# Output projection of the layer stage: from an FP32 product to three fp32r products of split rows and split weights

## The chip, the cores and the metric

The kernel runs on one core of one Trainium2 chip. The metric is the time of one execution on the device in microseconds; the figures are the median, the lowest and the highest of several executions. A profile is one more execution, recorded instruction by instruction; its times are those of that one execution. TensorE, the matrix engine, is called PE, its weight loads PEld; VectorE is DVE, ScalarE is ACT, GpSimd is POOL, SyncE is SP.

## The reference

The input is x, 16 sequences of 512 rows of 256 values. Four blocks follow one another, each with `x = layernorm(x + block(x))`:

```python
x = layernorm(x + L0_attn(x))   # windowed softmax attention, 16 heads of 64
x = layernorm(x + L0_ffn(x))    # int8 product, scales, bias
x = layernorm(x + L1_attn(x))   # linear attention, then gelu
x = layernorm(x + L1_ffn(x))    # ternary weights + low rank; relu squared

# L1_attn, the block that the change is in; per sequence, 1024 features = 8 chunks of 128
q, k, v = x @ wq + bq, x @ wk + bk, x @ wv + bv
Q, K = elu(q) + 1, elu(k) + 1
KV, Ksum = sum_s(K * v), sum_s(K)
attn = Q * KV / (Q * Ksum + 1e-6)
out = gelu(attn @ wo + bo)      # [512, 1024] @ [1024, 256]
```

All of it is float32, and the output is compared as such.

## The kernel before

The program has two stages. The first does the attention of block 0 for all sequences and takes the first 2000 us; the change doesn't touch it. The second, `run_layers`, does everything else, and begins at about 2004 us. SBUF is laid out anew for each stage.

**Tiles.** A sequence is 512 rows. Features lie on the 128 partitions, rows on the free side, so that k, v, q and up products have the form "128 features x 512 rows" in one PSUM bank each. The 1024 features of block 1's attention are `HC` = 8 chunks, the 1024 hidden features of its FFN `FC` = 8 chunks.

**Split products.** Most products are float32 products in three passes of the one-pass type fp32r: an operand a is split as `hi = round(a)` (written to an fp32r tile) and `lo = a - hi`, and hi*hi + lo*hi + hi*lo is summed in PSUM. Weights are split once, rows each time: ACT writes hi, DVE or POOL subtracts lo. Two products differ. The down product's weights are exact in fp32r, so it takes two parts (`rhi`, `rlo` with `proj_t`). The output projection, `pe_out` (L1138 through `pe_rows_product`), multiplies plain float32 tiles `at` and `wo`; the profile records two weight loads and two matmuls for each of its instructions, 8 for one chunk.

**Order.** `all_steps` runs b from -3 to 18 and c from 0 to 7; each engine walks through these steps in program order and meets the others at semaphores only. In step (b, c) of the steady state PE does, in this order: the k and the v product of sequence b+1, chunk c-1; at c = 0 a transposition of the next rows (`pe_y2`); the q product of (b, c); the out product of (b, c-2); at c = 0 the second `pe_y2`; the up product of sequence b-2, chunk c; at c = 7 `pe_y3`; the down product; the int8 work of a later sequence at c = 1 to 3; at c = 7 the second `pe_y3`. So four sequences are under way at once. K_BANK, V_BANK (used by v and by up in turn) and Q_BANK are single banks: the next product waits until DVE has read the last.

DVE does per step: `dve_k` (L1330), `dve_v` (L1337), `dve_at` (L1359, one tensor_scalar from `z`), at c = 0 the small sums (L1343 to L1350) and the low part of y2 (L1326), `dve_q` (L1365, then L1369), at c = 3 the inner part of the gelu (L1390, L1392) and at c = 4, 5 its last product (L1396), then the square (L1377, from the ReLU), at c = 7 the low part of y3 (L1326). Sums, statistics and copies for other sequences stand at the head of the step: L1403 at c = 1, L1384 at c = 2, L1321 at c = 3, 4, statistics (L66 to L78) at c = 4 to 6, L1311 and L1313 at c = 7.

ACT does: the square's high part (L1254); at c = 1, 7 L1207 or a normalisation (L93); ReLU and exponential of k (L1217, L1219); `act_q_inverse` of (b, c-1) (L1237, L1240), which writes `z` as the logarithm's exponential; the same pair for q; at c = 3, 4 three gelu gate passes (L1263 to L1267); at c = 5, 6 a normalisation; the ReLU of the up product (L1247).

POOL does: the square's low part (L1492), which the down product waits for; a bias sum at c = 0 (L1461), two down sums at c = 1 (L1485), two gelu passes at c = 2 (L1472), int8 sums at c = 3, 4 (L1468), two gelu sums at c = 5 (L1479), and 128x4 powers for the normalisations (L85, L87) at c = 4 to 6.

**Memory.** `ring` has 16 slots of 512 columns: two each for `at`, `z`, `r`, `sq`, `uq`, `uk`, one each for `ek`, `eq`, two for `gx` (the out product with bias). A buffer pair lets a step's producer run while the step before is still read.

**Prologue.** Steps b = -3 to -1 load and prepare weights beside the first rows: the ternary FFN weights on DVE (`dve_weights`: L830 to L861), wq's split (ACT L1019, POOL L1039), the rank product (`dve_rank`, L868). DMA loads are issued by SP, and by ACT before its first step; `wo` is the last of ACT's, and the first out product waits for it.

## Time and profile before

| | us |
|---|---|
| median of 3 runs | 3261.58 |
| lowest, highest | 3256.11, 3261.69 |
| the profiled execution | 3256.74 |
| its span, first to last instruction | 3254.9 |
| PE busy | 3055.7 (94%) |
| PE weight loads busy | 2500.4 (77%) |
| DVE busy | 2319.4 (71%) |
| ACT busy | 2161.6 (66%) |
| POOL busy | 1480.8 (45%) |
| out product, L1138, 1024 records | 242.4 busy, 379 ns each |
| down product, L1138, 512 + 512 records | 131.0 and 128.4 busy, 288 and 283 ns each |
| L1359 (`at`), 128 times | 78.1 busy, 610 ns each |
| L1492 (square's low part), 128 times | 170.9 busy, 1335 ns each |

How to read it: busy time is the union of an engine's instructions. Matmuls are pipelined: the record of one lasts longer than the time after which the next one starts, so the cost of a product is read from start to start. DVE and ACT instructions overlap by some 0.08 us when they follow each other without a wait. "[x <-ACT ...]" behind a row is idle time of the engine before the instruction, and what ended it.

### The profile page before, as it was taken

How to read it: one execution, taken by the hardware profiler on the slowest of the kernel's cores; microseconds unless marked ns; L12 is line 12 of the kernel's file. 1: busy time of each engine (PE TensorE's matmuls, PEld its weight loads, DVE VectorE, ACT ScalarE, POOL GpSimd, SP SyncE). 2: the span in 40 equal slices, each digit the busy share in tenths (PEclk: the TensorE clock that was granted, in tenths of full speed). 3: DMA queues.
4: the chain of work that ended last, by engine and by line, in shares of the span. 5: the costliest groups of instructions: out<-in, count | busy, mean ns of one | idle time of the engine just before them, and what ended most of it. 6: DMA issues, size and time to landing. Idle time of an engine off the chain costs nothing. (4 is left out here: it accounts for less than half of the span.)

```text
span 3254.9 us, 68762 instructions
## 1 busy us (share of the span) xinstructions
PE 3055.7 (94%) x20655; PEld 2500.4 (77%) x20655; DVE 2319.4 (71%) x6737; ACT 2161.6 (66%) x5660; POOL 1480.8 (45%) x2090
## 2 busy tenths in 40 slices
...
GB/s 80 8 14 21 9 14 21 9 14 21 10 14 21 9 14 21 10 14 21 9 14 21 2 27 79 27 7 7 14 17 16 20 14 14 14 14 14 7 14 20
DMA packets 50143, 58.60 MB, mean 18 GB/s; under 512 B 2849, under 2 KB 47921, under 8 KB 49473
## 3 DMA queue, kind: packets, MB, share of 16 engines
...
## 5 line engine op out<-in xcount | busy, mean ns | idle before, releaser
L577 POOL TENSOR_SCALAR a_ex<-a_ex,a_rc 128x384 f32<-128x384 f32 (+1 forms) x1024 | 533.8, 535 | 749.7 <-DVE a_rc L489 749.5
L386 ACT ACTIVATE a_ex<-a_sm,a_nm 128x384 f32<-128x384 f32 (+1 forms) x1024 | 572.5, 560 | 100.3 <-DVE a_nm L482 97.4
L482 DVE CUSTOM_DVE_ANT_0 a_sm<-sc,a_mask,a_rn 128x384 f32<-128x384 f32 (+1 forms) x1024 | 532.0, 545 | 45.3 <-PE sc L267 43.1
L1492 POOL TENSOR_TENSOR b_rlo<-b_ring,b_rhi 128x512 fp32r<-128x512 f32 x128 | 170.9, 1335 | 586.3 <-ACT b_rhi L1254 586.1
L392 ACT ACTIVATE a_pt<-tp 128x256 f32<-128x256 f32 (+1 forms) x512 | 220.1, 430 | 304.6 <-PE tp L278 304.6
L236 PE MATMUL pj<-a_whi,a_xhi 128*128 128x384 f32 x1024 | 397.1, 388 | 2.5 <-DVE a_rb L460 2.5
L561 POOL TENSOR_TENSOR a_qr<-a_ra,a_rb 128x256 f32<-128x256 f32 x512 | 367.5, 733 | 35.8 <-DVE a_rb L460 35.7
L267 PE MATMUL sc<-a_kT,a_qT 64*128 64x384 f32 (+1 forms) x2048 | 345.3, 455 | 2.4 <-DVE a_nm L482 0.9
L236 PE MATMUL pj<-a_whi,a_xlo 128*128 128x384 f32 x1024 | 346.4, 338 | 0.0
L236 PE MATMUL pj<-a_wlo,a_xhi 128*128 128x384 f32 x1024 | 345.2, 337 | 0.0
L288 PE MATMUL qk<-a_pt,a_v 128*64 128x128 f32 x5120 | 314.6, 278 | 31.7 <-issue 21.4
L288 PEld LDWEIGHTS qk<-a_pt,a_v 128*64 128x64 f32 x5120 | 285.8, 139 | 68.8 <-issue 66.8
L494 DVE COPY a_pt<-sc 128x256 f32<-128x256 f32 (+1 forms) x512 | 250.9, 490 | 58.5 <-PE sc L278 51.6
L458 DVE TENSOR_TENSOR a_ra<-pj,a_cos 128x256 f32<-128x256 f32 x512 | 215.1, 420 | 57.9 <-ACT a_sq L371 51.7
L267 PEld LDWEIGHTS sc<-a_kT,a_qT 64*128 64x128 f32 x2048 | 176.3, 186 | 96.0 <-issue 53.5
L278 PE MATMUL sc<-s_ident,a_ex 128*128 128x128 f32 x1280 | 232.2, 279 | 11.5 <-DVE a_pt L494 6.2
L1138 PE MATMUL out<-b_wo,b_ring 128*128 128x256 f32 x1024 | 242.4, 379 | 0.2 <-DVE b_ring L1384 0.2
L278 PE MATMUL tp<-s_ident,a_ex 128*128 128x128 f32 x1280 | 228.9, 277 | 4.8 <-ACT a_pt L392 4.1
L297 PE MATMUL qk<-a_wo,a_ot 128*128 128x256 f32 x1024 | 228.0, 381 | 1.5 <-DVE a_res L502 0.8
L1330 DVE SCALAR_TENSOR_TENSOR b_ring<-k,b_one_bk,b_ring 128x512 f32<-128x512 f32 x128 | 95.8, 748 | 178.0 <-ACT b_ring L1219 178.0
L297 PEld LDWEIGHTS qk<-a_wo,a_ot 128*128 128x128 f32 x1024 | 192.0, 190 | 35.1 <-issue 8.2
L1138 PEld LDWEIGHTS out<-b_wo,b_ring 128*128 128x128 f32 x1024 | 194.4, 190 | 31.3 <-issue 0.6
...
## 6 DMA issues: line engine op xcount, KB each, us to landing
...
```

The source lines that it names most:

```text
L236: last = e.matmul(PJ[t % 2][:, 0:3 * PW], a[:, c, t * P:(t + 1) * P], w[:, c, p * 3 * PW:(p + 1) * 3 * PW], start=c == 0 and k == 0, stop= ...
L267: e.matmul(SC[j][h][:, 0:width], qT[par][rows(h), (w + j) * WS:(w + j + 1) * WS], kT[par][rows(h), lo * WS:(hi + 1) * WS], start=True, sto ...
L278: last = e.transpose(TPS[h][:, k * P:(k + 1) * P], ex[h][w][:, k * P:(k + 1) * P], ident[:, :])
L288: last = e.matmul(QK[rows(h), w * WS:(w + 1) * WS], v[p % 4][:, k, rows(h)], pt[h][w][:, (k - lo) * P:(k - lo + 1) * P], start=k == lo, st ...
L297: last = e.matmul(QK[:, t * DIM:(t + 1) * DIM], ot[:, c, (2 * k + t) * P:(2 * k + t + 1) * P], wo[:, c, :], start=c == 0, stop=c == HC - 1)
L386: e.activation(ex[h][w][:, 0:width], sm[h][w % 2][:, 0:width], ACT.Exp, bias=nm[:, w, h:h + 1], scale=-1.0, accum_out=rs[:, w, h:h + 1]).t ...
L392: e.activation(pt[0][w][:, 0:width], TP[:, 0:width], ACT.Copy).then_inc(g['pt_act'], 1)
L482: e.tensor_tensor_reduce(out=sm[h][w % 2][:, 0:width], in0=SC[w % 2][h][:, 0:width], in1=mem['mask'][:, off:off + width], scale=rn[:, par, ...
L494: e.tensor_copy(pt[1][w][:, 0:width], TPS[1][:, 0:width]).then_inc(g['pt_dve'], 1)
L561: e.tensor_tensor(qr[par][:, t, :], ra[:, t % 2, :], rb[:, t % 2, :], ALU.add).then_inc(g['rot_pool'], 1)
L577: e.tensor_scalar(row, row, 0.0, rc[:, w, h:h + 1], ALU.add, ALU.mult).then_inc(g['exn_pool'], 1)
L1138: last = e.matmul(bank[:, t % 2 * DIM:(t % 2 + 1) * DIM], xt[:, t * P:(t + 1) * P], weight[:, c, :], start=c == 0 and t % 2 == 0 and k == ...
```

## The change

The output projection is computed as the other split products are: `at` is split into `ahi` and `alo`, `wo` into `wo_hi` and `wo_lo`, and a chunk's product takes three parts, 12 fp32r matmuls in place of 4 float32 ones.

- DVE computes `at` twice from `z`: once into `ahi` (fp32r) and once into `at` (float32). POOL subtracts: `alo = at - ahi` (`pool_at_low`), in each step, behind most of the step's other POOL work. PE waits for POOL's event instead of DVE's.
- `wo` is loaded into four ring slots and split in the prologue, in four pieces: ACT writes `wo_hi`, POOL `wo_lo`.
- The two new weight tiles and four new row tiles take memory. To make room, `at`, `z`, `r`, `uq`, `uk` get one buffer instead of two, `gx` and `dn` share one place, and prologue buffers move. Each brings a wait.
- `dve_rank` moves from step (-1, 3) to (-1, 6). In POOL's step the rstd of ln3 comes ahead of `pool_at_low`, the gelu's inner part behind it.

```diff
     def dve_rank(e):
+        e.wait_ge(w['wq_pool'], 4)
...
         if (b, c) == (-1, 3):
             dve_fc_difference(e)
-            dve_rank(e)
...
+        if (b, c) == (-1, 6):
+            dve_rank(e)
...
     def act_weights(e, b, c):
+        if out_weights_piece(b, c) is not None:
+            act_out_weights(e, out_weights_piece(b, c))
...
+    def out_weights_piece(b, c):
+        steps = ((-2, 7), (-1, 0), (-1, 5), (-1, 6))
+        return steps.index((b, c)) if (b, c) in steps else None
...
+    def act_out_weights(e, n):
+        e.wait_ge(i['wo'], 16)
+        e.activation(out_columns('wo_hi', n), out_columns('wo_raw', n), ACT.Copy).then_inc(w['wo_act'], 1)
+
+    def pool_out_weights(e, n):
+        e.wait_ge(w['wo_act'], n + 1)
+        e.tensor_tensor(out_columns('wo_lo', n), out_columns('wo_raw', n), out_columns('wo_hi', n).bitcast(F32),
+            ALU.subtract).then_inc(w['wo_pool'], 1)
...
     def pe_out(e, s, c):
-        e.wait_ge(g['at_dve'], HC * s + c + 1)
+        e.wait_ge(g['al_pool'], HC * s + c + 1)
         if (s, c) == (0, 0):
-            e.wait_ge(i['wo'], 16)
+            e.wait_ge(w['wo_pool'], 4)
             e.wait_ge(w['bu_dve'], 2)
         if c == 0 and due(s):
             e.wait_ge(g['o_dve'], 2 * s)
-        pe_rows_product(e, O, [(mem['at'][c % 2], mem['wo'])], c).then_inc(g['o_pe'], 1)
+        hi, lo = (mem['ahi'][c % 2], mem['alo'][c % 2])
+        pe_rows_product(e, O, [(hi, mem['wo_hi']), (lo, mem['wo_hi']), (hi, mem['wo_lo'])], c).then_inc(g['o_pe'],
+            1)
...
     def act_q(e, s, c):
         e.wait_ge(g['q_pe'], HC * s + c + 1)
+        if (s, c) == (0, 0):
+            e.wait_ge(w['wo_pool'], 4)
...
     def act_q_inverse(e, s, c):
-        if due(n - 1):
-            e.wait_ge(g['at_dve'], n - 1)
+        if due(n):
+            e.wait_ge(g['at_dve'], n)
...
     def act_relu(e, s, c):
-        if due(n - 1):
-            e.wait_ge(g['sq_dve'], n - 1)
+        if due(n):
+            e.wait_ge(g['sq_dve'], n)
...
     def dve_k(e, s, c):
         e.wait_ge(g['ke_act'], HC * s + c + 1)
+        if due(HC * s + c):
+            e.wait_ge(g['v_dve'], HC * s + c)
...
     def dve_at(e, s, c):
         if due(n - 1):
             e.wait_ge(g['o_pe'], n - 1)
-        e.tensor_scalar(mem['at'][c % 2], mem['z'][c % 2], mem['nc'][:, c:c + 1], mem['cc'][:, c:c + 1], ALU.mult,
-            ALU.add).then_inc(g['at_dve'], 1)
+        factor, term = (mem['nc'][:, c:c + 1], mem['cc'][:, c:c + 1])
+        e.tensor_scalar(mem['ahi'][c % 2], mem['z'], factor, term, ALU.mult, ALU.add)
+        if due(n):
+            e.wait_ge(g['al_pool'], n)
+        e.tensor_scalar(mem['at'], mem['z'], factor, term, ALU.mult, ALU.add).then_inc(g['at_dve'], 1)
...
     def dve_q(e, s, c):
-        if due(n - 1):
-            e.wait_ge(g['ql_act'], n - 1)
+        if due(n):
+            e.wait_ge(g['ql_act'], n)
...
     def dve_out_bias(e, s, k):
+        if k == 0 and due(s - 1):
+            e.wait_ge(g['y4_pool'], 2 * (s - 1))
...
+    def pool_at_low(e, s, c):
+        n = HC * s + c
+        e.wait_ge(g['at_dve'], n + 1)
+        if due(n - 1):
+            e.wait_ge(g['o_pe'], n - 1)
+        e.tensor_tensor(mem['alo'][c % 2], mem['at'], mem['ahi'][c % 2].bitcast(F32),
+            ALU.subtract).then_inc(g['al_pool'], 1)
...
     def pool_step(e, b, c):
-        if c == 2 and inside(b - 1):
-            for k in range(2):
-                pool_gelu_inner(e, b - 1, k)
...
+        if c == 6 and inside(b - 1):
+            n3.rstd(e, b - 1)
+        if inside(at[0]):
+            pool_at_low(e, *at)
+        if c == 2 and inside(b - 1):
+            for k in range(2):
+                pool_gelu_inner(e, b - 1, k)
         if c == 5 and inside(b + 2):
             n2.rstd(e, b + 2)
-        if c == 6 and inside(b - 1):
-            n3.rstd(e, b - 1)
+        if out_weights_piece(b, c) is not None:
+            pool_out_weights(e, out_weights_piece(b, c))
...
-            e.dma_start(mem['wo'][:, :, :], io['wo1'].rearrange('(c p) n -> p c n', p=P)).then_inc(i['wo'], 16)
+            e.dma_start(mem['wo_raw'], io['wo1'].rearrange('(c p) n -> p c n', p=P)).then_inc(i['wo'], 16)
...
-    for i, k in enumerate(('at', 'z', 'r', 'sq', 'uq', 'uk')):
-        mem[k] = [ring[:, 2 * i + j, :] for j in range(2)]
-    mem['ek'], mem['eq'] = (ring[:, i, :] for i in (12, 13))
-    mem['gx'] = ring[:, 14:16, :]
+    for i, k in enumerate(('at', 'z', 'uq', 'eq', 'r')):
+        mem[k] = ring[:, i, :]
+    mem['sq'] = [ring[:, i, :] for i in (5, 6)]
+    mem['uk'], mem['ek'] = (ring[:, i, :] for i in (7, 8))
+    mem['gx'] = mem['dn'] = ring[:, 9:11, :]
```

## Rows read from the trace of the kernel before

**Rows 1.** Busy time by stretch: start:end, length, engines (instructions), PE clock, DMA, GB/s.
```profile
2397.42:2469.68 72.26, 70.35 (x355) 58.24 (x354) 48.59 (x117) 55.62 (x90) 25.58 (x24) 1.00 0.05 15
```

**Rows 2.** Waits of PE in that stretch: us in total, times, longest.
```profile
PE v_up L1058 <- DVE b_ring L1377: 1.1, 1, 1.1
PE t L1052 <- DVE b_y3lo L1326: 0.6, 1, 0.6
PE v_up L1058 <- DVE b_ring L1337: 0.2, 1, 0.2
```

**Rows 3.** Order in time on PE, step (5, 3): start, us, engine, line, operation.
```profile
2428.28 1.89 PE L1138 MATMUL out<-b_wo,b_ring 128*128 128x256 f32 x8
...
2430.24 0.40 PE L1058 MATMUL v_up<-b_y3lo,b_fhi 128*128 128x512 f32 x1
...
2431.50 0.28 PE L1138 MATMUL down<-b_proj_t,b_rlo 128*128 128x256 f32 x1
2431.62 0.28 PE L1138 MATMUL down<-b_proj_t,b_rhi 128*128 128x256 f32 x1
```

**Rows 4.** Order in time on DVE and POOL, three places where they meet.
```profile
3158.30 1.50 DVE L1365 TENSOR_SCALAR b_ring<-b_ring 128x512 f32<-128x512 f32 x1
3156.80 2.72 POOL L1479 TENSOR_TENSOR b_y<-b_g,b_y 128x512 f32<-128x512 f32 x2
...
2037.10 0.88 DVE L843 SCALAR_TENSOR_TENSOR b_dn<-b_y,b_wst,b_g 128x256 f32<-128x256 f32 x2
2037.50 1.95 DVE L843 SCALAR_TENSOR_TENSOR b_dn<-b_y,b_wst,b_g 128x256 f32<-128x256 f32 x2
2037.87 1.29 POOL L1039 TENSOR_TENSOR b_wq_lo<-b_y,b_wq_hi 128x512 fp32r<-128x512 f32 x1 [8.81 <-ACT b_wq_hi L1019]
...
2460.81 0.69 DVE L1313 TENSOR_SCALAR b_qf<-b_qf 128x1024 f32<-128x1024 f32 x1
2460.86 1.79 POOL L1492 TENSOR_TENSOR b_rlo<-b_ring,b_rhi 128x512 fp32r<-128x512 f32 x1 [5.03 <-ACT b_rhi L1254]
```

**Rows 5.** Order in time: L1365 in step (5, 3), and how soon POOL follows DVE.
```profile
2429.86 0.43 DVE L1365 TENSOR_SCALAR b_ring<-b_ring 128x512 f32<-128x512 f32 x1 [0.74 <-ACT b_ring L1219]
...
2451.57 0.17 DVE L78 TENSOR_SCALAR b_ln_ve<-b_ln_mv 128x4 f32<-128x4 f32 x1
2451.81 1.02 POOL L85 TENSOR_TENSOR b_ln_rs<-b_ln_ve,b_half 128x4 f32<-128x4 f32 x1 [4.09 <-DVE b_ln_ve L78]
```

**Rows 6.** Order in time on DVE and PE, step (5, 0).
```profile
2401.96 0.55 DVE L1359 TENSOR_SCALAR b_ring<-b_ring,b_nc,b_cc 128x512 f32<-128x512 f32 x1
2402.42 0.20 DVE L1343 RECIPROCAL b_ki<-b_su 128x8 f32<-128x8 f32 x1
...
2402.68 0.17 DVE L1346 TENSOR_TENSOR b_kb<-b_kb,b_kv 128x8 f32<-128x8 f32 x1
...
2403.16 0.68 DVE L1326 TENSOR_TENSOR b_y2lo<-t,b_y2hi 128x512 fp32r<-128x512 f32 x1
...
2403.90 0.66 PE L1052 MATMUL t<-s_ident,b_y 128*128 128x128 f32 x4
```

**Rows 7.** Order in time on DVE and PE, step (5, 7).
```profile
2466.73 0.43 DVE L1365 TENSOR_SCALAR b_ring<-b_ring 128x512 f32<-128x512 f32 x1 [0.69 <-ACT b_ring L1219]
...
2468.53 0.68 DVE L1326 TENSOR_TENSOR b_y3lo<-t,b_y3hi 128x512 fp32r<-128x512 f32 x1
...
2469.27 0.66 PE L1052 MATMUL t<-s_ident,b_y 128*128 128x128 f32 x4 [0.63 <-DVE b_y3lo L1326]
```

**Rows 8.** The square on DVE: all from 2200 to 3000 us, and in step (5, 4).
```profile
L1377 DVE SCALAR_TENSOR_TENSOR b_ring<-v_up,b_ring 128x512 f32<-128x512 f32 x88 | 60.8, 691 | 59.4 <-ACT b_ring L1247 59.4
...
2442.51 0.69 DVE L1377 SCALAR_TENSOR_TENSOR b_ring<-v_up,b_ring 128x512 f32<-128x512 f32 x1 [0.20 <-ACT b_ring L1247]
```

**Rows 9.** The load of wo: kind, count, KB and us to landing; and its issue.
```profile
b_wo<-wo ACTq DMA_DIRECT2D x1, 1024.0 KB, 12.4
...
2010.10 1.16 ACTq L1570 DMA_DIRECT2D b_wo<-wo  x1
```

More of the change, by code:

```diff
@@ L1040, in pool_query_weights, with out_columns @@
             ALU.subtract).then_inc(w['wq_pool'], 1)
+    def out_weights_piece(b, c):
+        steps = ((-2, 7), (-1, 0), (-1, 5), (-1, 6))
+        return steps.index((b, c)) if (b, c) in steps else None
+    def out_columns(name, n):
+        rows = mem[name] if name == 'wo_raw' else mem[name][:, :, :]
+        return rows.rearrange('p c n -> p (c n)')[:, n * 512:(n + 1) * 512]
+    def act_out_weights(e, n):
[5 more added lines that the diff above has]
+            ALU.subtract).then_inc(w['wo_pool'], 1)
     def pool_begin(e):
@@ L1233, in act_q_inverse @@
         e.wait_ge(g['qu_dve'], n + 1)
-        if due(n - 1):
-            e.wait_ge(g['at_dve'], n - 1)
-        z = mem['z'][c % 2]
-        e.activation(z, mem['uq'][c % 2], ACT.Ln, bias=mem['eps'][:, 0:1],
+        if due(n):
+            e.wait_ge(g['at_dve'], n)
+        z = mem['z']
+        e.activation(z, mem['uq'], ACT.Ln, bias=mem['eps'][:, 0:1],
             scale=mem['su'][:, s % 2, c:c + 1]).then_inc(g['ql_act'], 1)
@@ L1244, in act_relu @@
         e.wait_ge(g['h_pe'], n + 1)
-        if due(n - 1):
-            e.wait_ge(g['sq_dve'], n - 1)
-        e.activation(mem['r'][c % 2], V_BANK[:, :], ACT.Relu).then_inc(g['r_act'], 1)
+        if due(n):
+            e.wait_ge(g['sq_dve'], n)
+        e.activation(mem['r'], V_BANK[:, :], ACT.Relu).then_inc(g['r_act'], 1)
     def act_square_high(e, s, c):
@@ L1376, in dve_square @@
             e.wait_ge(g['rl_pool'], n - 1)
[L1377 removed]
+        e.scalar_tensor_tensor(mem['sq'][c % 2], V_BANK[:, :], 0.0, mem['r'], ALU.max,
             ALU.mult).then_inc(g['sq_dve'], 1)
@@ L1495, in pool_step @@
     def pool_step(e, b, c):
-        square = square_unit(b, c)
+        square, at = (square_unit(b, c), at_unit(b, c))
         if inside(square[0]):
@@ L1587, in sb @@
         return stack.enter_context(nc.sbuf_tensor('b_' + name, shape, dt))
-    mem = {k: sb(k, v) for k, v in dict(wo=[P, HC, DIM], ring=[P, 16, S], y1=[P, TT, DIM], qf=[P, TT, DIM], ws=[P,
-        DIM], bo=[P, DIM], bias=[P, DIM], psc=[P, DIM], g1=[P, 2, S], g2=[P, 2, S], dn=[P, 2, S], half=[P, TT],
+    mem = {k: sb(k, v) for k, v in dict(ring=[P, 11, S], y1=[P, TT, DIM], qf=[P, TT, DIM], ws=[P,
+        DIM], bo=[P, DIM], bias=[P, DIM], psc=[P, DIM], g1=[P, 2, S], g2=[P, 2, S], half=[P, TT],
         eps=[P, 1], ln_eps=[P, 1], unround=[P, 1], xs=[P, 2], top=[P, 2], gate=[P, 1], wst=[P, 4, FC], nbq=[P, HC],
@@ L1601, in layers_memory @@
     mem['y3hi'], mem['y3lo'] = (sb(k, [P, DC, S], F32R) for k in ('y3hi', 'y3lo'))
-    for k in ('rhi', 'rlo'):
+    for k in ('rhi', 'rlo', 'ahi', 'alo'):
         mem[k] = [sb(f'{k}{i}', [P, S], F32R)[:, :] for i in range(2)]
+    mem['wo_hi'], mem['wo_lo'] = (sb(k, [P, HC, DIM], F32R) for k in ('wo_hi', 'wo_lo'))
     mem['w8raw'] = sb('w8raw', [P, DC, DIM // 4], INT32)
```

35 lines of the change are left out of this document (17 added, 18 removed).

## The prediction

> **What bounds the kernel now.** I read the view by stretches first, for the layers, which are all that the change touches. One sequence, from one k product at step c = 0 to the next, takes 72.26 us; in it PE is busy 70.35, DVE 48.59, ACT 55.62, POOL 25.58, and the granted clock is 1.00, the 2.4 GHz level [rows 1]. The reader is to see a PE that hardly rests and a POOL with two thirds of its time free. Then the waits of PE in that sequence: 1.9 us in three places, always for DVE: a v product waits for the square, a transposition for the low part of y3, an up product for the v reduction [rows 2]. So PE is the bound, but at three points of each sequence a chain through ACT and DVE is just as long as PE's work. What is won or lost on those chains counts as much as what PE wins.
>
> **What PE gains.** The out product starts at 2428.28 and the second matmul behind it at 2430.24 [rows 3]. A matmul of 512 columns takes 0.23 (twice the 0.12 between two records of the down product, which have 256 columns [rows 3]), so one out product takes 2430.24 - 0.23 - 2428.28 = 1.73 us. The new one is 12 matmuls of the form of the down product: 12 x 0.12 = 1.43. Gain 0.30 us, 128 times: 38 us if nothing else moved.
> The Trainium skill (FP8 and Floating Point Precision, on FP32) says that true FP32 takes four passes through the array. By that the old product would be 16 x 0.12 = 1.92 us and the gain 0.49; the row says 1.73, and the row decides.
>
> **What DVE gets.** `dve_at` becomes two tensor_scalar passes instead of one. One more costs 0.47: L1359 starts at 2401.96 and its follower at 2402.42 [rows 6]. No row shows a tensor_scalar that writes fp32r. The nearest, a tensor_tensor that does, lasts 0.68, with the same overlap of 0.08 that is 0.60 [rows 6]; so the bounds are 0.47 and 0.60. I take 0.47, since operation and operands are L1359's. Behind the old pass DVE idles 0.74 us until ACT's exponential of q is there, and then runs L1365 [rows 5]. The second pass fits into that gap, and by itself costs little.
>
> **What POOL gets, and the lock.** One 128x512 subtraction per chunk, 1.29 us like L1039 [rows 4]. POOL has the time. But the trace shows that POOL and DVE shut each other out. L1365, else 0.43, took 1.50 while two L1479 ran on POOL until 3159.52; it ended 0.28 after them [rows 4]. L843, which has two SBUF inputs, takes 0.88 for two, and took 1.95 for two when L1039 held POOL until 2039.16; it ended 0.29 after it. The other way round, POOL's L1492 took 1.79 when it began 0.05 behind DVE's L1313 [rows 4]. Whoever starts first keeps the other out.
> The Trainium skill (SBUF — State Buffer, Who interferes with whom) calls it an exclusive lock on the second port pair, between GpSimd and a DVE instruction in a two-port mode or with two SBUF inputs. The trace agrees: 1.50 beside 0.43.
>
> Now the race in each step. POOL starts 0.07 to 0.08 us after the end of the DVE instruction that releases it (L78 ends at 2451.74, L85 starts at 2451.81) [rows 5]. L1365 starts when ACT is ready. Times from the end of the old pass:
> - Step 3. The second pass ends at +0.47, POOL starts at +0.55, L1365 would come at +0.74 [rows 5]: too late. POOL ends at +1.84, L1365 at +2.12 instead of +1.17: shift 0.95. Behind it lie q, the inner part of the gelu, ACT's three gate passes, the ReLU and the square, for which PE's v product of step 4 already waits 1.1 us [rows 2]. Cost +0.95, and the 0.30 of steps 3 and 4 turn into waiting.
> - Step 7. L1365's idle time is 0.69, so POOL wins again. From 2466.73 on DVE has 0.43, 0.75 and 0.69 us of work without a gap, then L1326 at 2468.53 (low part of y3), for which PE's transposition waits until 2469.27 [rows 7]. Cost +0.95.
> - Step 0. Behind the pass stand the small sums. L1346 (two SBUF inputs) started 0.17 after L1359's end [rows 6]; now POOL starts 0.08 after the second pass and holds it until 1.37 after it. Shift 0.47 + 1.37 - 0.17 - 0.15 of L1346's own length, 1.52. L1326 behind it (low part of y2) ended at 2403.84, PE's transposition started at 2403.90 [rows 6]. PE now waits: +1.52, and this product's 0.30 is gone.
> - Steps 1 and 2. L1365 is late by 1.0 too, but its square has idle time before it (0.67 on average over the steps [rows 8]) and PE comes to the v product only after down and k, over 2 us of work. No cost; the two gains stay: -0.60.
> - Step 4. DVE has no idle time there: L1365 follows at once and beats POOL. But POOL's subtraction then runs into L1396 (two SBUF inputs), and the square after it has 0.20 of idle time [rows 8]. 0.47 for the pass plus up to 0.5 for the lock, less 0.20, and step 5, where POOL's two L1479 come later for the same reason, hands it on to PE's v product of step 6. Bounds 0 and 1.0; I take +0.5.
> - Steps 5 and 6. Nothing new; their gains go into a chain of ACT (three normalisations) that ends in step 7's wait.
> Sum: 1.52 - 0.60 + 0.95 + 0.50 + 0.95 = +3.3 us, so 72.3 becomes 75.6.
>
> **The other edits.** Single buffers for z, uq, uk, r and at: each new wait is for something a whole step old (72.26 / 8 = 9 us) or already waited for on the same engine; that step hides it: 0. gx on dn's memory: DVE's L1384, and k and v behind it, wait for POOL's down sum of the step before, 2.6 us of its 9: 0; without that cover up to 1.3 once a sequence. POOL's order: the rstd of ln3 stays ahead of the subtraction, the gelu's part goes behind it and is needed a step later: 0. PE waits for POOL instead of DVE, but one step after the pass: 0.
> The split of wo adds 4 ACT and 4 POOL passes to the prologue. Its DMA lands 12.4 us after its issue at 2010.10 [rows 9], before ACT is through with the first rows. The last two POOL passes meet L861 and L1311, which are DVE work of the locking kind, at a time when DVE is the bound; `dve_rank` costs the same at its new place, and the q splits that it waits for are done by then. Bounds -1.3 (the rank copies leave a tight place) and +2.6 (two POOL passes in full, 2 x 1.29); I take +1.5.
>
> **Sum.** 13 full sequences (b = 2 to 14) x 3.3 = 43. The first two, without up and down: up to 14 gains of 0.30 against one step 0 and one step 7: +2 (-2 to +5). The last, with long waits for DVE: +3 (0 to +6). Prologue +1.5. Together +50 on the profiled execution's 3256.7: 3307. The median shown, 3261.6, lies 4.9 above that execution; I put half of it on top: **3309 us**.
> If a pass that writes fp32r takes 0.60, POOL starts at +0.68 and L1365 in step 7 (0.69) draws level: that term goes, 13 x 0.95 = 12 us: 3297. With all bounds at the upper end (13 x 0.5 + 7): 3322.
>
> **Rivals.**
> 1. *The lock costs nothing on the path* (POOL wakes later, or DVE is let in first): step 0 keeps +0.47 and the two gains -0.60: -0.13 per sequence, prologue and ends as above, 3257 to 3264: no change. Against it: L1365 at 1.50.
> 2. *The second pass hides in step 0 too*: 13 x 0.60 to 0.90 less the prologue: 3248 to 3254, faster.
> 3. *PE is the bound throughout*, its 1.9 us of waits only leftovers: 3261.6 - 38 = 3223. Against it: the three waits end chains in which no out product stands.
> By the four passes of the page named above this rival would give 128 x 0.49 less, 3199.
> 4. *The change doesn't do what it says*: the 12 matmuls go at the old product's 0.216, since weight loads show: 2.6 us, +0.86 in 2 to 4 steps, with the lock and without the gains 3337 to 3360. Against it: the down product has such loads at a pace of 0.12.
> The sign hangs on one point: whether POOL's subtraction starts within 0.27 us of the second pass's end in step 3.
>
> **Chances.** Forecast (3285 to 3326) 0.70; the lock in some steps only (3268 to 3285) 0.07; rival 1 0.09; rival 2 0.06; rival 3 0.04; rival 4 0.04. A measurement of this kernel tells about 0.2% (6.5 us) from no change. Faster 0.12, within 0.08, slower 0.80. The range leaves out rivals 2, 3 and 4 and half of rival 1: 3262 to 3326; the forecast's own is 3285 to 3326.
>
> **What would show it.** L1365's successor at about 1.4 us in steps 1, 2, 3, 6 and 7 and at 0.43 in steps 4 and 5; an out product of 1.43 us; a sequence of 75 to 76 us; waits of PE of about 1 us or more in steps 0 and 7 and 2 in step 4. I am wrong if L1365 keeps 0.43 in step 3, or a sequence takes under 73 us.

## The result

| | before | after |
|---|---|---|
| median | 3258.85 (3253.94 to 3261.69, 4 executions) | 3315.94 (3314.98 to 3316.87, 4 executions) |
| profiled execution, its span | 3256.74, 3254.9 | 3316.87, 3315.1 |

After to before: 1.0177, 95% interval 1.0159 to 1.0194. The change costs 57 us. The prediction was 3309, range 3262 to 3326, slower with 0.80.

**One sequence.** A sequence is read as the stretch from PE's k product at the head of one step (b, 0) to the next, as in [rows 1]. In the trace of after it is b = 4 and b = 5, and two microseconds within b = 5 (columns as in [rows 1]: length; busy time and count of PE, PEld, DVE, ACT, POOL; granted clock):

```profile
2343.26:2419.06 75.80, 68.12 (x387) 58.01 (x386) 57.80 (x125) 55.46 (x90) 36.44 (x32) 1.00 0.05 15
2419.06:2495.53 76.47, 69.44 (x387) 59.06 (x386) 59.06 (x125) 55.48 (x90) 36.05 (x32) 0.98 0.05 14
2461.00:2463.00 2.00, 2.00 (x6) 1.52 (x6) 1.93 (x9) 1.17 (x2) 1.82 (x2) 0.50 0.00 0
```

Against [rows 1] PE does 2.2 us less in b = 4 (70.35 to 68.12), DVE 9.2 more, POOL 10.9 more, and the sequence is 3.5 us longer. The second row has a part that no row of before had between b = 2 and 14: the granted clock falls to 0.50 for a few microseconds.

**Which step.** The steps of b = 4, one row each:

```profile
2343.26:2354.06 10.80, 9.14 (x55) 7.82 (x54) 7.30 (x17) 6.28 (x10) 4.60 (x3) 1.00 0.01 2
2354.06:2362.42 8.36, 8.36 (x54) 7.28 (x53) 6.27 (x11) 6.12 (x9) 5.10 (x4) 1.00 0.00 0
2362.42:2370.80 8.38, 8.38 (x52) 7.27 (x50) 6.84 (x13) 7.11 (x11) 3.89 (x4) 1.00 0.00 0
2370.80:2379.17 8.37, 8.37 (x52) 7.27 (x49) 5.91 (x11) 4.64 (x7) 3.84 (x3) 1.00 0.01 2
2379.17:2390.32 11.15, 8.54 (x48) 6.96 (x45) 9.37 (x25) 9.25 (x15) 5.18 (x5) 1.00 0.15 47
2390.32:2398.24 7.92, 7.92 (x46) 6.89 (x45) 6.51 (x13) 6.74 (x12) 5.20 (x4) 1.00 0.01 2
2398.24:2407.49 9.25, 8.19 (x46) 6.82 (x45) 7.76 (x28) 6.79 (x13) 5.23 (x6) 1.00 0.17 58
2407.49:2419.06 11.57, 9.22 (x54) 7.70 (x53) 7.84 (x13) 8.54 (x15) 3.41 (x3) 1.00 0.00 1
```

In steps 1, 2, 3 and 5 PE is busy all the time (8.38 of 8.38): there it is the bound, and there the cheaper product shows. In 0, 4, 6 and 7 its busy time is 1 to 2.6 us less than the step. Cut the same way, the kernel before (b = 5, the stretch of [rows 1]) has 9.32, 8.65, 8.66, 8.66, 9.92, 8.24, 8.42, 10.39; its steps 0, 3, 4, 6 and 7:

```profile
2397.42:2406.74 9.32, 9.32 (x51) 7.76 (x50) 5.81 (x16) 6.28 (x10) 3.33 (x2) 1.00 0.00 0
...
2424.05:2432.71 8.66, 8.66 (x48) 7.36 (x45) 5.71 (x12) 5.18 (x8) 2.56 (x2) 1.00 0.01 2
2432.71:2442.63 9.92, 8.85 (x44) 6.89 (x41) 7.98 (x23) 8.71 (x15) 3.78 (x4) 1.00 0.17 53
...
2450.87:2459.29 8.42, 8.42 (x43) 6.91 (x41) 6.21 (x25) 6.84 (x12) 3.68 (x5) 1.00 0.19 64
2459.29:2469.68 10.39, 9.55 (x50) 7.64 (x49) 6.47 (x12) 8.27 (x15) 2.12 (x2) 1.00 0.00 1
```

So steps 1, 2, 3 and 5 won 0.3 each, and 0, 4, 6 and 7 lost 1.5, 1.2, 0.8 and 1.2. Step 6 of b = 4 is longer than most: its median from b = 2 to 13 is 8.91, so that it usually loses 0.5.

**For whom PE waits.** Waits of PE in b = 4 (total, times, longest), to be held against [rows 2]:

```profile
PE v_up L1079 <- DVE b_ring L1407: 3.3, 2, 2.3
PE t L1073 <- DVE b_y2lo L1351: 1.7, 1, 1.7
PE t L1073 <- DVE b_y3lo L1351: 1.6, 1, 1.6
PE v_up L1079 <- DVE b_ring L1364: 1.1, 2, 0.8
```

L1407 is the square (L1377 before), L1351 the low parts (L1326), L1364 `dve_v`. 1.9 us of waiting have become 7.7, all of it for DVE, as before. The wait for y2's low part, in step 0, and a second one for the square, in step 6 (1.1 us here), are new; none is for POOL.

**The lock.** Step 3 of b = 4: the two passes, POOL's subtraction (L1524), and the first operation on q (L1395, L1365 before) with its successor:

```profile
2375.33 0.55 DVE L1387 TENSOR_SCALAR b_ahi<-b_ring,b_nc,b_cc 128x512 fp32r<-128x512 f32 x1
2375.79 0.54 DVE L1390 TENSOR_SCALAR b_ring<-b_ring,b_nc,b_cc 128x512 f32<-128x512 f32 x1
2376.61 1.37 DVE L1395 TENSOR_SCALAR b_ring<-b_ring 128x512 f32<-128x512 f32 x1 [0.28 <-ACT b_ring L1242]
2378.02 0.75 DVE L1399 SCALAR_TENSOR_TENSOR b_ring<-q,b_one_bq,b_ring 128x512 f32<-128x512 f32 x1
...
2376.41 1.29 POOL L1524 TENSOR_TENSOR b_alo<-b_ring,b_ahi 128x512 fp32r<-128x512 f32 x1 [2.10 <-DVE b_ring L1390]
```

L1390 ends at 2376.33, POOL starts 0.08 later, L1395 comes 0.20 behind POOL and lasts 1.37 instead of 0.43, until 0.28 after POOL's end. In step 5 DVE is first and POOL is the one that is drawn out:

```profile
2396.11 0.53 DVE L1390 TENSOR_SCALAR b_ring<-b_ring,b_nc,b_cc 128x512 f32<-128x512 f32 x1
2396.57 0.41 DVE L1395 TENSOR_SCALAR b_ring<-b_ring 128x512 f32<-128x512 f32 x1
...
2396.72 1.41 POOL L1524 TENSOR_TENSOR b_alo<-b_ring,b_ahi 128x512 fp32r<-128x512 f32 x1 [0.81 <-DVE b_ring L1390]
```

In step 0 it is one of the small sums that is held (L1373, `kb + kv`, 8 columns: 1.20 us), and behind it the low part of y2 for which PE waits 1.7 us. The first sum with two SBUF inputs, L1371, still slipped in 0.05 ahead of POOL:

```profile
2348.26 0.54 DVE L1390 TENSOR_SCALAR b_ring<-b_ring,b_nc,b_cc 128x512 f32<-128x512 f32 x1
2348.72 0.20 DVE L1370 RECIPROCAL b_ki<-b_su 128x8 f32<-128x8 f32 x1
2348.83 0.12 DVE L1371 TENSOR_TENSOR b_kb<-b_su,b_bv 128x8 f32<-128x8 f32 x1
2348.98 1.20 DVE L1373 TENSOR_TENSOR b_kb<-b_kb,b_kv 128x8 f32<-128x8 f32 x1
...
2348.88 1.27 POOL L1524 TENSOR_TENSOR b_alo<-b_ring,b_ahi 128x512 fp32r<-128x512 f32 x1 [2.29 <-DVE b_ring L1390]
```

Over the program L1395 has 411/1368/1462 ns (lowest, median, highest); L1365 had a median of 427. The out product is 12 matmuls 0.12 apart:

```profile
2394.82 0.28 PE L1159 MATMUL out<-b_wo_hi,b_ahi 128*128 128x256 f32 x1
...
2395.78 0.28 PE L1159 MATMUL out<-b_wo_lo,b_ahi 128*128 128x256 f32 x1
```

(The second row is its ninth.) The Trainium skill (SBUF — State Buffer, Who interferes with whom) lets whoever issues first keep the shared port pair for its whole instruction; these three places agree, in both directions.

**The clock.** The v product of step 4, now in b = 5 (PE's rows; the bracket is the wait before the instruction and its releaser):

```profile
2458.90 0.50 PE L1079 MATMUL v_up<-b_y2hi,s_w_hi 128*128 128x512 f32 x1 [2.28 <-DVE b_ring L1407]
2459.24 0.39 PE L1079 MATMUL v_up<-b_y2lo,s_w_hi 128*128 128x512 f32 x1
...
2460.79 0.63 PE L1079 MATMUL q<-b_y2hi,b_wq_hi 128*128 128x512 f32 x1
2461.22 0.63 PE L1079 MATMUL q<-b_y2lo,b_wq_hi 128*128 128x512 f32 x1
```

About a microsecond after a wait of 2.28 us the matmuls start 0.43 apart instead of 0.23: the granted clock is 0.50 (1.2 GHz) for some 3.4 us. In b = 4 the same wait of 2.28 stands there and no fall follows. Between b = 2 and 14 eight sequences have such a stretch, and each begins between 0.3 us before and 1.5 us after the end of that wait (2.69 us in b = 14). Step 4 then lasts 12.0 to 12.1 instead of 11.15. q is late by it; in five of the eight, b = 5 among them, L1395 then comes so late (0.42 after the second pass) that POOL wins in step 4 too. That adds little: in b = 11 POOL doesn't win, and step 4 lasts 12.1 all the same.

**Where the 60 us of the two profiles lie** (the layers' start is SP's first load there, the other borders are the k products at (0, 0), (2, 0) and (15, 0)): the attention stage, whose code is the same, ends 5.1 later; the layers' start to (0, 0) 63.0 to 65.5, +2.5; the first two sequences 113.8 to 116.6, +2.7; the 13 full ones 936.5 to 985.8, +49.3; the end 136.7 to 137.2, +0.6.

### The profile page after: what moved, and what is told of

It reads as the page before. It is cut to its first block and busy times, and to the rows that moved or that the text cites. A ratio compares the mean times of both kernels' runs of the same rounds, so it can differ in the third digit from the quotient of the medians.

```text
span 3315.1 us, 70305 instructions
## 1 busy us (share of the span) xinstructions
PE 3037.6 (92%) x21167; PEld 2509.0 (76%) x21167; DVE 2469.6 (74%) x6865; ACT 2161.4 (65%) x5664; POOL 1651.5 (50%) x2222
## 5 line engine op out<-in xcount | busy, mean ns | idle before, releaser
L1524 POOL TENSOR_TENSOR b_alo<-b_ring,b_ahi 128x512 fp32r<-128x512 f32 x128 | 169.5, 1325 | 276.1 <-DVE b_ring L1390 276.1
L460 DVE TENSOR_TENSOR a_rb<-pj,a_sin 128x256 f32<-128x256 f32 x512 | 211.9, 414 | 0.0
```

## The experiments

Columns: the median of one sequence (b = 2 to 13), and the steps in that order, all by PE's k products. "Total" is one execution where no ratio stands beside it, and else a median and its ratio to the kernel before, run beside it.

| | 0 | 1 | 2 | 3 | 4 | 5 | 6 | 7 | sequence | total |
|---|---|---|---|---|---|---|---|---|---|---|
| before | 9.3 | 8.7 | 8.7 | 8.7 | 9.9 | 8.2 | 8.4 | 10.4 | 72.2 | 3259 |
| e4: old product, new buffers | 9.3 | 8.7 | 8.7 | 8.7 | 9.9 | 8.2 | 8.4 | 10.4 | 72.2 | 3259.8 |
| e3: new product alone | 9.3 | 8.4 | 8.4 | 8.4 | 10.2 | 7.9 | 8.4 | 10.6 | 71.7 | 3255.7 |
| e1: and the second pass | 9.8 | 8.4 | 8.4 | 8.4 | 10.2 | 7.9 | 8.6 | 10.6 | 72.3 | 3261.9 |
| e2: and POOL's subtraction | 10.1 | 8.4 | 8.4 | 8.4 | 10.4 | 7.9 | 9.1 | 10.9 | 73.5 | 3275.5 |
| after: both | 10.8 | 8.4 | 8.4 | 8.4 | 11.2/12.1 | 7.9 | 8.9 | 11.6 | 75.5/76.5 | 3316 |
| e7: PE's wait filled | 10.8 | 8.4 | 8.4 | 8.4 | 11.2 | 7.9 | 8.9 | 11.6 | 75.5 | 3308.3 |
| e8: after, old product | 10.8 | 8.6 | 8.7 | 8.7 | 10.9/12.1 | 8.3 | 8.9 | 11.3 | 76.0/77.0 | 3324.5 |
| e5: POOL behind q | 9.8 | 8.4 | 8.4 | 8.4 | 11.2/12.1 | 7.9 | 8.7 | 10.6 | 73.4/74.2 | 3290.0, 1.0081 |
| e9: and behind the gelu's inner part | 9.8 | 8.4 | 8.4 | 8.4 | 10.2 | 7.9 | 8.9 | 10.6 | 72.5 | 3266.9, 1.0014 |

(With a slash: without and with a fall of the clock in the sequence.)

### Which part costs what: e1 to e4

Without POOL's subtraction (e1):

```diff
-        if inside(at[0]):
-            pool_at_low(e, *at)
...
-        e.wait_ge(g['al_pool'], HC * s + c + 1)
+        e.wait_ge(g['at_dve'], HC * s + c + 1)
...
-        hi, lo = (mem['ahi'][c % 2], mem['alo'][c % 2])
+        hi = lo = mem['ahi'][c % 2]
```

> The changed kernel without POOL's subtraction of the row remainder; DVE keeps both passes, and the product takes the high part twice, so it has the same twelve matmuls. What is left out: the low part of the rows. Read from the full sequences b = 2 to 14 (before 72.3 us, after 75.8 with an undisturbed clock). Theory (the lock between POOL and DVE is the larger part of the loss): nothing holds L1395 (0.43 everywhere) nor the small sums of step 0. What is left is the second pass alone: step 0 +0.47, steps 1 and 2 -0.58, steps 3 and 4 about +0.47 and +0.2, step 7 +0.47, together about +1.0: 73.3 us a sequence, and some 3280 us in all. Rival A (the second pass is the loss, or the rate of DVE's work as a whole): stays at 75 to 76. Rival B (the second pass hides everywhere once the lock is gone): 71.7 us.

72.29 us, 3261.9 in all: less than expected. The 0.47 of the pass shows in step 0 (9.31 to 9.77, against e3) and 0.18 in step 6, but not in 3 and 7. That expectation had an error of its own: L1395 comes 0.7 us after the old pass, and the second pass fits into that gap. The lock is needed for the pass to cost anything there. L1395 (L1393 in e1) stays at 409 to 430 ns throughout. Rival A falls, and so does rival B, since step 0 does pay for the pass.

Without the second pass (e2), POOL subtracting `ahi` from itself:

```diff
-        e.tensor_scalar(mem['ahi'][c % 2], mem['z'], factor, term, ALU.mult, ALU.add)
-        if due(n):
-            e.wait_ge(g['al_pool'], n)
-        e.tensor_scalar(mem['at'], mem['z'], factor, term, ALU.mult, ALU.add).then_inc(g['at_dve'], 1)
+        e.tensor_scalar(mem['ahi'][c % 2], mem['z'], factor, term, ALU.mult, ALU.add).then_inc(g['at_dve'], 1)
```

> The changed kernel without DVE's second pass: POOL subtracts the high part from itself, as long a pass as before, 0.08 us after the first pass of DVE. What is left out: the low part of the rows is zero. Theory (lock): POOL still gets in ahead of L1395 in steps 3 and 7, where it comes 0.7 us after the pass, and ahead of the small sums in step 0; each loss is smaller by the 0.47 of the pass: step 0 +1.05, steps 1 and 2 -0.58, step 3 +0.48, step 4 about +0.2, step 7 +0.48 (to +0.7), together +1.6 to +1.9: 74.0 us a sequence, L1395's successor at 1.3 to 1.5 in steps 1, 2, 3, 6 and 7. Rival A (the second pass is the loss): 72 us or less.

73.54 us. Steps 0, 4, 6 and 7 are longer than in e3, as expected, but less so, and rival A (72 us or less) falls. Step 3 of b = 5:

```profile
2440.06 0.66 DVE L1392 TENSOR_SCALAR b_ring<-b_ring 128x512 f32<-128x512 f32 x1 [0.74 <-ACT b_ring L1242]
...
2439.40 1.04 POOL L1521 TENSOR_TENSOR b_alo<-b_ahi 128x512 fp32r<-128x512 f32 x1 [1.64 <-DVE b_ahi L1387]
```

With the same tile on both sides POOL took 1.04, not 1.29, so this run understates the lock by 0.25 in each held step. L1392 (L1395 of after) lasted 0.66: held 0.23, and again until 0.28 after POOL's end. With 1.29 the delay would have been 0.48, as expected; that is an estimate, not a run. The other sign that was named was missed: L1392 was put at 1.3 to 1.5 us in steps 1, 2, 3, 6 and 7, and has medians of 0.65 to 0.75 there. Without the second pass POOL starts 0.66 ahead of it in step 3, not 0.20, and most of POOL's operation is over when it comes.

Neither (e3: both edits together, the first pass and the three-part product left), and the old product on top (e4):

```diff
-        pe_rows_product(e, O, [(hi, mem['wo_hi']), (lo, mem['wo_hi']), (hi, mem['wo_lo'])], c).then_inc(g['o_pe'],
+        pe_rows_product(e, O, [(hi.bitcast(F32), mem['wo_hi'][:, :, :].bitcast(F32))], c).then_inc(g['o_pe'],
```

> The changed kernel with neither the second pass nor POOL's subtraction: the cheaper product (high part of the rows in both places), the single buffers, the new order of POOL and the split of the weights in the prologue stay. What is left out: the low part of the rows. Theory: only steps in which PE is the bound give their 0.3 us back, two to three of eight: 71.5 us a sequence (71.2 to 71.7), in all 3250 us with the prologue's loss. Rival C (PE is the bound throughout and its waits are leftovers): 72.3 - 2.4 = 69.9 us a sequence. Together with the two kernels before, the pass and the lock add up or don't: if their costs are a plain sum, after = this + (e1 - this) + (e2 - this).

> As the kernel before in its work per step (one FP32 product, one pass of DVE, no subtraction of POOL), but with the single buffers, the shared memory of gx and dn, POOL's new order and the split of the weights: the edits that the prediction costed at nothing in the sequences, and the prologue. What is left out: the low parts of rows and weights. Theory: 72.3 us a sequence as before (72.2 to 72.5), the prologue +1.5 to +2.5: about 3260 us in all. Rival D (one of the new waits of the single buffers or of gx counts): 73 to 74 us a sequence, and a new releaser in the waits of PE or ACT.

One sequence of e4, e3, e1 and e2, in this order, each from its own trace:

```profile
2403.29:2475.50 72.21, 70.32 (x355) 58.23 (x354) 48.52 (x117) 55.60 (x90) 25.57 (x24) 1.00 0.05 15
```

```profile
2403.19:2474.86 71.67, 68.15 (x388) 57.97 (x386) 48.56 (x117) 55.62 (x90) 25.59 (x24) 1.00 0.05 15
```

```profile
2406.71:2479.00 72.29, 68.10 (x387) 58.00 (x386) 52.20 (x125) 55.61 (x90) 25.61 (x24) 1.00 0.05 15
```

```profile
2407.39:2480.93 73.54, 68.11 (x387) 57.97 (x386) 51.36 (x117) 55.62 (x90) 34.06 (x32) 1.00 0.05 15
```

e4 repeats [rows 1] within 0.1 in every column: the single buffers, the shared place of gx and dn and POOL's order cost nothing, and rival D falls. From e4 to e3 PE's work drops by 2.2 us and the sequence by 0.54: the rest turned into waits of steps 4 (9.9 to 10.2) and 7 (10.4 to 10.6). Rival C, PE as the bound throughout, falls. From e3, the pass adds 0.6, POOL's subtraction 1.9, and both together 3.8 (75.5 - 71.7). They are no plain sum. 0.25 in each held step is POOL's shorter operation in e2. The rest follows from the starts, though no run shows it by itself: the pass alone is hidden in front of L1395, but it puts off POOL's start by 0.47, and with it the end of the lock.

The same question with one part instead of three (e11, `[(hi, mem['wo_hi'])]` in e3's kernel):

> The kernel with the product alone, its product cut from three parts to one (4 matmuls, 0.48 us, instead of 12, 1.43). What is left out: the low parts of rows and weights. Theory (PE is the bound only in steps 1, 2, 3 and 5): the gain of 0.95 stays in steps 1 and 2 as far as ACT allows (some 6.9 us of ACT a step), those of steps 3 and 5 turn into waits of steps 4 and 7 for the square: 71.65 - 1.9 = 69.7 to 70.5 us a sequence. Rival C (PE is the bound throughout): 71.65 - 7.6 = 64.0.

Two sequences have 70.4 us, as expected; the other ten have 71.0 to 73.0, mean 71.8, 3248.9 in all. Rival C (64.0) falls once more. 0.95 us less per product is worth nothing in the mean (71.8 beside e3's 71.7): PE waits 2.28 us for the square in step 4 and 1.90 for `dve_v` in step 7, and in b = 5, with 72.6 us, the clock fell behind both:

```profile
2437.83 0.50 PE L1079 MATMUL v_up<-b_y2hi,s_w_hi 128*128 128x512 f32 x1 [2.28 <-DVE b_ring L1404]
...
2468.81 0.72 PE L1079 MATMUL v_up<-b_y3hi,b_fhi 128*128 128x512 f32 x1 [1.90 <-DVE b_ring L1364]
```

The changed kernel with the old product (e8, the diff of e4 alone):

> The changed kernel with all work of DVE and POOL, but PE makes one FP32 product of the high parts, 1.73 us instead of 1.43. What is left out: the low parts of rows and weights. Theory: the 0.3 us count only in steps 1, 2, 3 and 5 and are taken off the waits of steps 4 and 7, as between the kernels with and without the new product (72.23 to 71.65): +0.6 us a sequence beside the changed kernel, 76.4 with an undisturbed clock, and shorter waits of PE (2.28 falls to about 2.0), with which the clock may fall less often. Rival C (PE is the bound): +2.4 us a sequence, 78.2 or more.

76.0 us without a fall, 77.0 with one: +0.5, as from e3 to e4. Steps 1, 2, 3, 5 are longer by 0.3, 4 and 7 shorter by 0.3. The product's gain is real and has the same size with the lock as without it.

### The clock: e7

```diff
     def pe_v(e, s, c):
+        if inside(s - 3) and c == 3:
+            e.wait_ge(g['qu_dve'], HC * (s - 1) + 4)
+            for k in range(8):
+                e.matmul(Q_BANK[:, :], mem['wq_hi'][:, 0, 0:P], mem['y2hi'][s % 2][:, 0, :], start=True, stop=True)
         if inside(s - 3):
```

> The changed kernel, with 8 matmuls (128x128 by 128x512, 0.23 apart, 1.85 us) of no use into q's bank, ahead of the v product of step 4, where PE otherwise waits 2.28 us for the square; q's own product overwrites them. Theory F (the granted clock falls to 0.50 in half of the sequences because of this wait, and that is what lengthens step 4 from 11.15 to 12.1): no stretch at 0.50 between b = 2 and 14, step 4 at 11.15 in all, the period 75.5 to 75.8 in all, some 6 us less in all, although PE has more to do. Rival G (the fall comes from elsewhere, and the waits only go beside it): stretches at 0.50 stay, median of step 4 near 12.

Step 4 of b = 5, PE:

```profile
2451.98 2.01 PE L1145 MATMUL q<-b_y2hi,b_wq_hi 128*128 128x512 f32 x8
2454.42 0.50 PE L1079 MATMUL v_up<-b_y2hi,s_w_hi 128*128 128x512 f32 x1 [0.43 <-DVE b_ring L1411]
```

But for one at the very start of b = 2 (at 2188.5, in the step's first microsecond) there is no stretch at 0.50 between b = 2 and 14. Nearly every sequence takes 75.5 us (75.47 to 75.52 in ten of twelve), step 4 is 11.16 throughout, and the program took 3308.3: eight useless matmuls a sequence made it faster, by 6.8 us in the 13 full sequences (985.8 to 979.1). Theory F holds: the wait is what brought the clock down, and rival G falls. Why only about every second wait does so is left open. It also gives the clean price of the change: 979.1 - 936.5 = 42.6 for 13 sequences.

### Where POOL may stand: e5, e6, e9, e10, e12

```diff
     def pool_at_low(e, s, c):
         n = HC * s + c
         e.wait_ge(g['at_dve'], n + 1)
+        if inside((n + 1) // HC):
+            e.wait_ge(g['qu_dve'], n + 2)
```

> The whole change, with one more wait: POOL's subtraction starts only when DVE's second operation on q (L1399) of the same step is done. Nothing is left out. Theory (what costs is that POOL gets in ahead of L1395 and of the small sums of step 0): L1395 takes 0.43 everywhere, step 0 is 9.77, steps 1 to 3 8.38, step 4 10.2, step 7 10.6 as in the kernel with the pass alone, 72.3 to 72.8 us a sequence (POOL may still get between the passes of the inner part of the gelu in step 3, where the square has 1.45 us of idle time), 3262 to 3268 in all, about the time of the kernel before. Rival E (any subtraction of POOL costs, wherever it stands, since 1.3 us of the ports are taken from DVE eight times a sequence): 74 us or more, 3285 and above.

L1395 takes 410 to 430 ns in all 128 cases, steps 0 and 7 are those of e1 (9.8, 10.6), and the kernel costs 28 us more than the kernel before run beside it (3262.2), where after cost 57. But step 4 is 11.2, and 12.1 with a fall of the clock, not 10.2. Step 3 of b = 5 in e5:

```profile
2448.53 0.68 DVE L1422 TENSOR_TENSOR b_g<-b_g,b_ring 128x512 f32<-128x512 f32 x1
2449.24 1.39 DVE L1424 TENSOR_SCALAR b_g<-b_g 128x512 f32<-128x512 f32 x1
...
2448.74 1.61 POOL L1526 TENSOR_TENSOR b_alo<-b_ring,b_ahi 128x512 fp32r<-128x512 f32 x1 [3.04 <-issue]
```

POOL, first held by L1422, gets in between it and L1424, which is held to 1.39. ACT's gate, the ReLU and the square come 0.96 later, PE's v product waits 2.30, and in eight of the twelve sequences the clock falls. By its numbers (74 us or more, 3285 and above) rival E fits this run better than the theory. Otherwise the theory was wrong by one place where the same lock bites again. One more wait tells these apart (e9):

```diff
+        if c == 2 and inside(s - 1):
+            e.wait_ge(g['gc_dve'], 4 * s)
```

> The run with POOL's subtraction behind q, and in step 3 alone it also waits for the last L1424 (the inner part of the gelu). Nothing is left out. Theory (in the run before, step 4 was 12.1 instead of 10.2 because the subtraction of step 3 started between L1422 and L1424, held L1424 to 1.39 instead of 0.43, and ACT's gate, the ReLU and the square behind it came 0.96 later; PE's 2.30 us of waiting then brought the clock down): L1424 back at 0.43, the v product of step 4 waits about 1.35, no stretch at 0.50 between b = 2 and 14, step 4 at 10.2 to 10.5, 72.3 to 72.6 us a sequence, 3262 to 3268 in all, within 0.3% of the kernel before. Rival E (any subtraction costs): step 4 stays at 11 or more, 73.4 us a sequence or more.

Its step 3:

```profile
2444.89 0.68 DVE L1422 TENSOR_TENSOR b_g<-b_g,b_ring 128x512 f32<-128x512 f32 x1
2445.61 0.43 DVE L1424 TENSOR_SCALAR b_g<-b_g 128x512 f32<-128x512 f32 x1
...
2447.32 1.27 POOL L1528 TENSOR_TENSOR b_alo<-b_ring,b_ahi 128x512 fp32r<-128x512 f32 x1 [5.24 <-DVE b_g L1424]
```

72.5 us a sequence, step 4 at 10.2, 3266.9 in all, ratio 1.0014 (1.0003 to 1.0024). The clock falls at the very start of b = 2 and once in b = 14 and nowhere between. POOL does the same 36.5 us of work a sequence as in after. All work of the change is there, and two waits of POOL have brought its cost from 57 to 6 us, each against the kernel before run beside it (the ratio from 1.0177 to 1.0014): it is where POOL's subtraction stands that costs. Rival E falls.

e9 lies 0.85 us a sequence above e3, all in steps 0 and 6; 0.46 and 0.18 of it are the second pass, as in e1. In e6 POOL makes the unrounded rows as well (0.77 to 1.0 us, in front of its subtraction), and `nc` and `cc` have two buffers:

```diff
     def pool_at_low(e, s, c):
...
+        e.tensor_scalar(mem['at'], mem['z'], mem['nc'][:, s % 2, c:c + 1], mem['cc'][:, s % 2, c:c + 1], ALU.mult,
+            ALU.add).then_inc(g['ap_pool'], 1)
+        e.wait_ge(g['ap_pool'], n + 1)
         e.tensor_tensor(mem['alo'][c % 2], mem['at'], mem['ahi'][c % 2].bitcast(F32),
```

> The whole change, with the subtraction behind q as in the run beside it, and the pass that makes the unrounded rows on POOL too, in front of its subtraction (POOL's tensor_scalar of this size takes 0.65 in L1504; nc and cc get two buffers). DVE has one pass left. Nothing is left out. Theory: 0.6 us less than the run beside it, since the pass costs 0.46 in step 0 and 0.18 in step 6: 71.7 to 72.2 us a sequence, 3254 to 3260 in all, at or just below the kernel before. Rival E (POOL's work itself costs, two operations more than one): longer than the run beside it.

72.8 us, or 73.8 with a fall of the clock, 3281.8 in all, 1.0048 (1.0028 to 1.0068): step 0 is back at 9.3, but step 4 is 10.7, or 11.7 with a fall, since in step 3 POOL's pass held L1423 (L1424 in e5) to 0.89 and its subtraction held the second product of the gelu's inner part (L1421, L1422 in e5) to 1.78, and step 6 is 9.1. So two operations of POOL without e9's wait cost less in step 4 than one in e5, and the forecast of 71.7 to 72.2 was missed for the same reason as e5's. Rival E (longer than e5) falls. e10 adds e9's wait and moves POOL's rstd of ln2 ahead of the two in step 5:

> The run with the unrounded rows and the subtraction both on POOL, behind q, and in step 3 behind the last L1424; in step 5 POOL's rstd of ln2 goes ahead of the two, since they had held L77 there. Nothing is left out. Theory: only the work of the kernel with the product alone is left on the path: steps 9.3, 8.4, 8.4, 8.4, 10.2, 7.9, 8.5 to 8.7, 10.6, 71.7 to 71.9 us a sequence, no fall of the clock between b = 2 and 14, 3254 to 3260 in all: the kernel before less 0.1 to 0.2%. Rival E (any subtraction costs): 72.8 or more. Rival H (in step 5 POOL is through too late, and PE's out product of step 6 waits for it): step 6 at 9 or more, with a wait of PE for POOL.

72.0 us a sequence, but 3267.5 in all, 1.0023 (1.0012 to 1.0033). Rival E (72.8) falls; rival H doesn't show in the full sequences (step 6 at 8.9, one wait of PE for POOL, of 0.18 us). What the sequences gained was lost in the first two, 123.8 us instead of 116.6. There are no up and down products there, steps last 6 us, and PE does wait for POOL (waits of PE from (0, 0) to (2, 0)):

```profile
PE out L1159 <- POOL b_alo L1532: 10.5, 6, 3.8
```

So e12 leaves those waits, and the rstd's new place, out of the first two sequences:

> The run with rows and subtraction both on POOL (72.0 us a sequence), but in the first two sequences, which have no up and down products and steps of only 6 us, POOL waits for nothing of q and the rstd of ln2 stays behind the subtraction; there PE had waited 10.5 us in 6 waits of the out product for POOL. Nothing is left out. Theory: the two first sequences fall from 123.8 to 113 to 117 us, the full ones stay at 72.0, together 7 to 10 us less than that run, 3257 to 3262: no difference to the kernel before that can be measured. Rival I (those waits only stood beside a slow stretch of the clock, which comes at another place): 120 us or more for the first two.

116.4 us for the first two, 72.0 for the others, 3256.5 in all: 0.9991 of the kernel before, interval 0.9980 to 1.0002. Rival I (120 us or more for the first two) falls. A sequence costs 0.2 us less than before, and the program as a whole can't be told from it. No version here beats the kernel before by a measurable amount; e3, which makes no low part at all, puts what this product can win, with the rest of the program as it is, at some 0.55 us a sequence.

## Why the prediction was right, and where it was off

- **Direction and size.** Forecast 3309, measured 3315.9. Its 3.3 us for a full sequence stands against 3.27 (75.5 - 72.23) with an undisturbed clock, its 43 for 13 of them against 42.6 in e7. The total hides more: between the two profiles, where 50 were forecast, lie 60.2, of which 5.1 are the attention stage, that nothing was changed in, and 6.8 the clock. Of the terms below, nothing was counted for step 5, which won 0.3, and as much too little for step 7, where it comes back as waiting; the sum doesn't show it.
- **Price of the product.** Twelve matmuls 0.12 apart, 1.43 from start to start, as forecast from the down product [rows 3]. Rival 4 fell with that.
- **Step 0, +1.52.** Measured +1.48. Held was the small sum that the prediction named (L1346, now L1373); the one ahead of it with two SBUF inputs, of which the prediction said nothing, escaped by 0.05. (Its row has 0.17 for that sum's own length, not 0.15; by that the term is 1.50.)
- **Steps 1 and 2, -0.60.** Measured -0.29 and -0.28. L1395 was held there too, and the square's slack took it, as said.
- **Steps 3 and 4.** Forecast +0.95 for step 3, landing in step 4's wait; measured -0.29 and +1.23, together +0.94. The point on which the sign was put, whether POOL starts within 0.27 us of the pass's end, came out at 0.08 [rows 5].
- **Step 4's own +0.50, handed on to step 6.** Measured in step 6: +0.49 in most sequences (8.42 to 8.91), +0.83 in b = 4. It was taken from bounds of 0 and 1.0, so that this close a hit is luck. Steps 5 and 6 together are +0.20 (+0.51 in b = 4), for step 5 won 0.29. POOL's two gelu sums of step 5 (L1511, L1479 before) come later and hold the first pass: L1387 lasts 1.41 there instead of 0.54.
- **Step 7, +0.95.** Measured +1.18. e3 without any lock has 10.63 against 10.39: that is 0.24 of the 0.3 that PE won in step 5 and gave back as waiting here. The prediction said that those gains go into step 7's wait, and counted neither the gain nor the wait; the lock's part is 0.94.
- **The signs.** L1395 at 1.4 us in steps 1, 2, 3, 6 and 7 was said: between b = 2 and 13 it took 1.37 to 1.43 in all of steps 1, 2, 3 and 7 and 1.46 in ten of twelve steps 6 (in b = 4 and 9 it went ahead of POOL there). It stayed at 0.41 to 0.43 in step 5 and in step 4, except in the five sequences named under the clock. PE's wait in step 4 was put at 2, and was 2.28.
- **What was missing: the clock.** Nothing in the trace of before let it fall between b = 2 and 14; its longest wait of PE there was 1.1 us [rows 2]. The forecast made a wait of 2 us out of it and didn't ask what such a wait does to PE. It cost 6.8 us in 13 sequences. No term of the range stood for it. The result lies 6.9 above 3309, but that these two are alike is chance: the other errors (the attention stage +5.1, the prologue +1.0, the first two sequences +0.7, the last -2.4, and the 2.5 put on top for the median, which came out 0.9 below its profile) happen to cancel.
- **The other edits.** Nothing in the sequences, confirmed by e4. The prologue was put at +1.5: from the start of the layers to (0, 0) before took 63.0 us, after 65.5, and the other kernels with the same split of wo lie from 62.1 (e8, e9) to 65.3 (e12). The places at which the clock is at 0.50 there differ from trace to trace, so that only "-0.9 to +2.5" can be said; no run shows that the split costs anything. The first two sequences, +2, were +2.7; the last, +3, was +0.6.
- **Rivals.** 1 (the lock costs nothing) is refuted by e9 beside after: 72.5 and 75.5 with the same work. 2 (the second pass hides in step 0) by e1: +0.46 there. 3 (PE the bound) by e3 and e11.
